# Attention with group norm over 32 batches: first input tile in two transfers, last products reordered, last output in four parts

## What is computed

```
q = conv1x1(Wq, bq, y);  k = conv1x1(Wk, bk, y);  v = conv1x1(Wv, bv, x)
scores = einsum('bhdl,bhel->bhde', q, k) / sqrt(E)        # per head, 16 x 16
attn = softmax(scores, axis=-1)
out = einsum('bhde,bhel->bhdl', attn, v).reshape(B, E, Lx)
o = conv1x1(Wo, bo, out) + x
o_hat = (o - mean(o)) * rsqrt(var(o) + EPS)               # over all of a batch
return o_hat * gn_w + gn_b
```

## Time and profile before

| What | us |
|---|---|
| Median of three executions | 175.67 |
| Lowest and highest of them | 175.47, 176.19 |
| The profiled execution, its own time | 175.87 |
| Its span in the trace | 174.1 |
| Busy in the span: PE, DVE, ACT, POOL | 163.0, 151.8, 135.8, 112.4 |

### The profile page before, as it was taken

One profiled execution on the slowest core, in us unless ns is written; L12 is line 12 of the kernel. 1 busy time (PEld: TensorE's weight loads), 2 busy tenths in 40 slices (PEclk: granted clock), 3 DMA queues, 4 the chain that ended last, 5 costly groups with the idle time before them and its releaser, 6 DMA issues. The chain is left out here.

```text
span 174.1 us, 4168 instructions
## 1 busy us (share of the span) xinstructions
PE 163.0 (94%) x997; PEld 129.2 (74%) x997; DVE 151.8 (87%) x555; ACT 135.8 (78%) x356; POOL 112.4 (65%) x166
## 2 busy tenths in 40 slices
PE   7989999999999999999999999999999999999730
PEld 7877888877777888877777778888777777785410
DVE  1786999999998999999999999999999999976551
ACT  4656588998878888798888888888988888776442
POOL 3287677877866777776787677767778777741020
PEclk9999999999999999999999999999999999999995
DMA  6998778999899999989999999999999866622223
GB/s 206 409 416 339 254 224 322 328 334 334 279 355 336 311 330 321 332 308 342 334 314 325 356 324 326 313 333 330 330 339 327 297 237 241 242 121 120 121 115 126
DMA packets 14265, 50.70 MB, mean 291 GB/s; under 512 B 1712, under 2 KB 1712, under 8 KB 14256
## 3 DMA queue, kind: packets, MB, share of 16 engines
q1 hardware_dynamic: 13968, 50.34, 81.0%
q10 hardware_dynamic: 288, 0.27, 0.5%
HBM read 33.82 MB, written 16.78 MB: 291 GB/s over the span
## 5 line engine op out<-in xcount | busy, mean ns | idle before, releaser
L514 PE MATMUL o_ps<-x_sb,m_sb 128*128 128x512 f32 x128 | 63.1, 615 | 0.0
L431 DVE TENSOR_TENSOR hl_sb<-y_sb,hl_sb 128x512 fp32r<-128x512 f32 x64 | 47.9, 749 | 1.7 <-ACT hl_sb L326 1.0
L271 POOL TENSOR_TENSOR rstd<-veps,nhalf 128x1 f32<-128x1 f32 x32 | 28.2, 882 | 24.5 <-DVE veps L436 24.5
L326 ACT CAST hl_sb<-y_sb 128x512 fp32r<-128x512 f32 x64 | 39.5, 620 | 1.8 <-DMA y_sb<-in_ctx_dram 1.8
L514 PE MATMUL g_ps<-hl_sb 128*128 128x258 f32 x256 | 38.6, 293 | 0.0
L366 ACT ACTIVATE out_sb<-o_ps,shift,gain 128x1024 f32<-128x1024 f32 (+1 forms) x32 | 38.3, 1197 | 0.1
L300 POOL TENSOR_TENSOR lsuma<-hl_sb 128x256 f32<-128x256 f32 x31 | 23.2, 749 | 22.9 <-DVE hl_sb L431 22.9
L514 PEld LDWEIGHTS o_ps<-x_sb,m_sb 128*128 128x128 f32 x128 | 22.1, 191 | 14.9 <-issue 14.0
L514 PEld LDWEIGHTS g_ps<-hl_sb 128*128 128x128 f32 x256 | 32.8, 190 | 0.0
L321 ACT ACTIVATE a_sb<-sc_sb,smin 128x128 f32<-128x128 f32 x32 | 12.9, 402 | 16.8 <-DVE smin L422 16.7
L287 POOL TENSOR_TENSOR lsum<-lsuma,lsumb 128x256 f32<-128x256 f32 x31 | 22.8, 737 | 4.1
(11 more groups left out here) (64 smaller groups left out, 297.6 us busy)
## 6 DMA issues: line engine op xcount, KB each, us to landing
y_sb<-in_ctx_dram SPq DMA_DIRECT2D x32, 512.0 KB, 5.1
x_sb<-in_x_dram SPq DMA_DIRECT2D x32, 512.0 KB, 5.6
out_dram<-out_sb SPq DMA_DIRECT2D x31, 512.0 KB, 4.8
out_dram<-out_sb SPq DMA_DIRECT2D x2, 256.0 KB, 2.2
w_in<-in_weights_dram ACTq DMA_DIRECT2D x1, 256.0 KB, 5.4
cols<-in_columns_dram ACTq DMA_DIRECT2D x1, 3.0 KB, 3.3
```

What stands on the lines that cost most here:

```text
L271: nc.gpsimd.tensor_tensor(rstd[:, h1:h1 + 1], veps[:, h1:h1 + 1], nhalf[:, :], ALU.pow).then_inc(rstd_ready, 1)
L326: nc.scalar.copy(hl_sb[:, k, chunks, 0:C], y_sb[:, k, chunks, :]).then_inc(h_ready, 1)
L431: nc.vector.tensor_tensor(hl_sb[:, ky, chunks, C:2 * C], y_sb[:, ky, chunks, :], hl_sb[:, ky, chunks, 0:C].bitcast(F32), ALU.subtract).the ...
L514: return nc.tensor.matmul(dst, lhsT, rhs, start=start, stop=stop, **more)
```

## The change

It alters six things:

1. The first `y` tile arrives in two transfers of 256 KB, by columns; the first has a semaphore of its own, `y_first`. ACT rounds the first half on the first, and waits for the second before the second half.
2. `w_in` is issued by SP behind the second `y` tile, instead of by ACT. DVE makes `wqT` in step 2, behind the rest of the second half of tile 1.
3. One warm-up product less, and no two idle products behind the row product.
4. In step 2, DVE makes `k0` behind `p_sb` instead of ahead of it.
5. In step 34, PE puts batch 31's `softmax_product` between the two x products of batch 30, the folded product behind them, and the first x product of batch 31 ahead of batch 30's `mean`. In step 35 it runs batch 31's second x product ahead of batch 30's `variance`, and DVE makes `veps` between the two statistics instead of ahead of both.
6. ACT and DVE each normalise the last batch in two quarters of 256 columns, and SP sends four transfers of 128 KB, in the order ACT, DVE, ACT, DVE.

```
-WARM_UP = 8
+WARM_UP = 7
...
-            for k in range(UNROLL):
+            part = HALF
+            sp.dma_start(y_slot(0)[:, 0:part], batch_y(0)[:, 0:part]).then_inc(y_first, 16)
+            sp.dma_start(y_slot(0)[:, part:L], batch_y(0)[:, part:L]).then_inc(y_in[0], 16)
+            sp.dma_start(y_slot(1), batch_y(1)).then_inc(y_in[1], 16)
+            sp.dma_start(w_in[:, :, :].rearrange("p w c -> p (w c)"), weights).then_inc(w_loaded, 16)
+            for k in range(2, UNROLL):
                 sp.dma_start(y_slot(k), batch_y(k)).then_inc(y_in[k], 16)
...
-                    for half, done in ((0, normed), (1, normed_dve)):
-                        part = slice(half * HALF, (half + 1) * HALF)
-                        sp.wait_ge(done, B if half == 0 else 1)
+                    for j in range(2):
+                        part = slice(j * QUARTER, (j + 1) * QUARTER)
+                        sp.wait_ge(normed, B + j)
+                        sp.dma_start(batch(out, B - 1)[:, part], out_sb[:, ko, part]).then_inc(out_done[ko], 16)
+                        part = slice(HALF + j * QUARTER, HALF + (j + 1) * QUARTER)
+                        sp.wait_ge(normed_dve, 1 + j)
                         sp.dma_start(batch(out, B - 1)[:, part], out_sb[:, ko, part]).then_inc(out_done[ko], 16)
...
-            act.dma_start(w_in[:, :, :].rearrange("p w c -> p (w c)"), weights).then_inc(w_loaded, 16)
...
-                if has(t, 5):
+                if has(t, 5) and not is_step(t, RUSH + 1):
                     variance()
...
                     nc.vector.bn_stats(bn[:, h, 0, :], o_ps[:, h, 0:HALF])
+                    if is_step(t, RUSH + 1):
+                        variance()
...
-            keep_busy(FILL)
```

More of the change, by code:

```diff
@@ L328, in step @@
                 if has(t, 0):
-                    act.wait_ge(y_in[k], slot_count(t0, k, 0))
+                    if is_step(t, 0):
+                        act.wait_ge(y_first, 16)
+                    else:
+                        act.wait_ge(y_in[k], slot_count(t0, k, 0))
                     if exists(t, 4):
@@ L364, in step @@
                         act.wait_ge(out_done[ko], slot_count(t0, k, 9))
-                    part = slice(0, HALF if is_step(t, LAST) else L)
-                    nc.scalar.activation(out_sb[:, ko, part], o_ps[:, h1, part], ACT.Identity,
-                                         bias=shift[:, h1:h1 + 1], scale=gain[:, h1:h1 + 1]).then_inc(normed, 1)
+                    parts = (slice(0, QUARTER), slice(QUARTER, HALF)) if is_step(t, LAST) else (slice(0, L),)
+                    for part in parts:
+                        nc.scalar.activation(out_sb[:, ko, part], o_ps[:, h1, part], ACT.Identity,
+                                             bias=shift[:, h1:h1 + 1], scale=gain[:, h1:h1 + 1]).then_inc(normed, 1)
                 ahead = is_step(t, 0) or is_step(t, 1)
                 if ahead:
+                    if is_step(t, 0):
+                        act.wait_ge(y_in[k], 16)
                     round_half(1)
@@ L441, in step @@
                     rest_half(-1, 1)
+                if is_step(t, 2):
+                    dve.wait_ge(w_loaded, 16)
+                    nc.vector.tensor_scalar(wqT[:, :], w_in[:, 0, :], -SCALE, None, ALU.mult).then_inc(const_dve, 1)
                 if has(t, 2):
@@ L470, in step @@
                                                    in1=p_ps, op0=ALU.mult, op1=ALU.add).then_inc(p_copied, 1)
+                if is_step(t, 2):
+                    nc.vector.scalar_tensor_tensor(out=k0[:, :], in0=bkB[:, :], scalar=bq_col[:, :],
+                                                   in1=mask[:, :, :].rearrange("p h d -> p (h d)"),
+                                                   op0=ALU.mult, op1=ALU.add).then_inc(const_dve, 1)
                 if has(t, 4):
@@ L500, in step @@
                     dve.wait_ge(out_done[ko], slot_count(t0, k, 9))
-                    nc.vector.tensor_scalar(out_sb[:, ko, HALF:L], o_ps[:, h1, HALF:L], gain[:, h1:h1 + 1],
-                                            shift[:, h1:h1 + 1], ALU.mult, ALU.add).then_inc(normed_dve, 1)
+                    for part in (slice(HALF, HALF + QUARTER), slice(HALF + QUARTER, L)):
+                        nc.vector.tensor_scalar(out_sb[:, ko, part], o_ps[:, h1, part], gain[:, h1:h1 + 1],
+                                                shift[:, h1:h1 + 1], ALU.mult, ALU.add).then_inc(normed_dve, 1)
             step(0, 0)
             step(0, 1)
-            dve.wait_ge(w_loaded, 16)
-            nc.vector.tensor_scalar(wqT[:, :], w_in[:, 0, :], -SCALE, None, ALU.mult).then_inc(const_dve, 1)
             pipeline(dve, step, begin=2)
@@ L609, in step @@
                     last.then_inc(hl_ready, 1)
-                if has(t, 3):
-                    pe.wait_ge(r_copied, t - 2)
-                    product(m_ps[:, 0:E], wv, r_sb[:, :])
-                    product(m_ps[:, E:E + 1], r_sb[:, :], bv).then_inc(m_ready, 1)
+                if has(t, 3) and not is_step(t, RUSH):
+                    folded_product()
                 if has(t, 4):
```

43 lines of the change are left out of this document (27 added, 16 removed).

## The result

The changed kernel takes 177.53 us (median of 6 runs, 176.85 to 179.52) beside 175.66 us for the kernel before (6 runs, 175.46 to 176.19). The ratio is 1.0095, 95% interval 1.0060 to 1.0129: **slower by about 1%**, where 175.1 was forecast with a range to 175.7.

What follows compares the result with a forecast made beforehand. PE alone bounds the gapless middle, so only start and end can gain. Profiled: 175.87 - 0.65 (start) + 0.05 (steps 34 and 35) + 0.0 (last output) = 175.27; from the median, 175.67 - 0.6, rounded to 175.1 us; range 174.4 to 175.7.

Steps and rivals of the forecast that it cites:

- `cols` and tile 0: Start, transfers: first half of tile 0 on ACT at 3.45, 0.6 us sooner; `cols` on DVE at 3.6 instead of 4.24.
- The rival of an unmoved `cols`: Start: `cols` stays at 4.24, only the idle passes are saved, -0.43 us, 175.3; chance 0.13.
- The start of PE: Row product at 4.2, Gram from 5.2, four passes at the lower clock; products with ones at 6.6 instead of 7.28, -0.65 us.
- the first rival: Start: PE's clock is up before 5.2, so 7.28 becomes 6.2, -1.1 us, 174.6 to 174.8; chance 0.20.
- The chain of step 1: Ones, `b2_sb`, transpose, `g_sb` and second Gram keep their old lengths, so it adds nothing to the sum.
- Tile 1: Start, ACT: with the row product 0.57 us sooner, tile 1 is cast at 5.8 instead of 6.36.
- The third rival: Start: thinner PE work makes the clock rise only after the second Gram, +2.6 - 0.6 us, 177.7; chance 0.06.
- Steps 34 and 35: New order near the end: gain in front is lost in DVE's queue, +0.05 us, between -0.1 and +0.15.
- The last output: Four transfers: issue +0.6, transfer -0.3, old queueing of halves some 0.3; sum 0.0 us, between -0.2 and +0.3.
- `k0`, `wqT`, `w_in`: Moves at the start: `w_in` and `wqT` cost nothing; `k0` costs 0 to 0.3 us, taken as 0.

Runs made afterwards that it cites:

- e15: Kernel before with tile 0 cut in two by partitions (rows of 4 KB), ACT waiting for both parts: 178.54 us, ratio 1.0101.
- e3: Kernel before with tile 0 in two transfers by columns and the weights on SP behind tile 1: 175.82 us, ratio 0.9991.
- e8: Changed kernel with eight warm-up products, the idle products back and the last output in two halves: 176.33 us, ratio 1.0050.
- e6: Kernel before with only tile 0 in two transfers by columns, weights left on ACT: 176.24 us, ratio 1.0042.
- e1: Changed kernel with eight warm-up products and the idle products behind the row product again: 177.04 us, ratio 1.0072.
- e13: Changed kernel with four idle products behind the ones products of step 1, where PE paused: 177.33 us, ratio 1.0089.
- e2: Kernel before with seven warm-up products instead of eight and no two idle products: 175.38 us, three of 12 runs at 178.01 to 179.23.
- e10: Changed kernel with tile 0 in one transfer again and `k0` and `wqT` in their old places: 175.73 us, ratio 1.0010.
- e4: Kernel before with only the new order of steps 34 and 35: 175.71 us, ratio 0.9991.
- e5: Kernel before with only the last output in four parts: 176.38 us, ratio 1.0028.
- e7: Kernel before with only the weights moved to SP behind tile 1: 175.71 us, ratio 1.0003.
- e14: Kernel before with the two idle products moved behind the ones products of step 1, plus the new order of steps 34 and 35: 175.26 us, ratio 0.9968.
- e9: Kernel before with the two idle products moved from behind the row product to behind the ones products of step 1: 175.45 us, ratio 0.9981.
- e11: Changed kernel with ACT copying `b2_sb` between its two casts of tile 1 in step 1: 177.91 us, ratio 1.0129.
- e12: Changed kernel with tile 1 issued by ACT behind `cols` instead of by SP: 177.65 us, ratio 1.0102.

## Why the prediction was wrong, point by point

- **`cols` and tile 0: right.** ACT's cast at 3.56 (3.45 forecast), `diag` at 3.74 (3.6), the row product at 4.28 (4.2). The rival of an unmoved `cols` is out. Why it moved is less sure than the forecast had it: in e15 `cols` had landed at 3.03, ahead of the first half of tile 0 (4.36), so it does not always wait for the tile's first transfer.
- **The start of PE: better than forecast.** The clock was up at 4.66, so the Gram was done sooner and the ones started at 6.20, not 6.6. That is the mechanism of the first rival (7.28 "becomes 6.2"), and the gain at this place is its 1.1 us.
- **The chain of step 1: the step that failed.** "Then the chain of step 1 (ones, `b2_sb`, transpose, `g_sb`, Gram 1) has its old lengths", and of `w_in` and `wqT` that "both cost nothing". From the ones to the second Gram it took 3.74 instead of 2.32, and the Gram 0.68 more. Three terms stood at nothing in the sum: the wait for `b2_sb` behind a late tile 1, `wqT` ahead of `g_sb`, and a clock that falls back.
- **Tile 1.** "The cast of tile 1 at 5.8 instead of 6.36" took for granted that the tile lands as before (5.52, which left 0.3 us of room). It was cast at 6.55. I had read the earlier trace rows for `cols` and the first half, not for the transfer behind them. That the split makes the tile late is shown: all eight kernels with tile 0 whole have it at 5.4 to 5.7, all eight cut by columns at 5.8 to 7.5. That this alone costs the time is not: e3 has it at 6.48 and is as fast as before. Why the engines trail is not shown. The rule in the Trainium skill's "DMA: Bandwidth & Descriptors", section "Rules for kernel authors", is about two transfers to disjoint partition halves, for which it advises one transfer over all 128 partitions. The prediction stretched it to halves by columns and weighed it for the first half alone, which did land 0.5 us sooner; the loss was in the transfer behind. For partition halves e15 bears it out: tile 0 came at 6.25 instead of 4.04.
- **In-order ACT.** The copy of `b2_sb`, which needs nothing of tile 1, is queued behind both its casts. I named this queue only for the case that the tile is there. It turns a late tile into a pause of PE of 0.76 (after, e8) or 1.39 (e6), and into none beyond the old 0.35 where the ones come late enough (e3, e1).
- **The clock.** The third rival, with a chance of 0.06, gave 177.7, nearly the measured 177.53, but by another course: it let the clock rise late. It rose early and fell back at 8.07, behind the pause; that the number is so near is luck. The argument against it, that PE's stream "stays unbroken to the end of the first Gram", was true, but the break came right behind. e13 has no low stretch with the pause filled, but its profiled execution had an early tile 1, so this is a hint and no proof. e6 and e8 show that a pause need not turn the clock (1.39 and 0.76 us, clock kept in the profiled execution), where PE had been given its idle products before. e2 shows that without the three products it can rise late: the third rival's course, seen in the one long execution that was profiled. That missing idle products and a pause together turn it in the changed kernel is argued; e10, without the idle products and with no longer pause than before, kept it. The edits done alone moved the median by -0.55 (e2), -0.11 (e3), -0.05 (e4) and +0.45 (e5), -0.26 in sum; the whole change moved it by +1.87. Missing from that sum are the moves of `k0` and `wqT`.
- **Steps 34 and 35.** Forecast +0.05, measured -0.19 and -0.18. `m_sb` came 0.23 later (0.3 forecast), the mean as forecast (4.70 behind batch 30's product). The term off is DVE's stretch from mean to `vrow`, 0.79 instead of 0.89, and `x` of batch 31 0.1 sooner than thought.
- **The last output.** Forecast 0.0, measured +0.48 and +0.45. The last issue was to come 0.6 later and its transfer to be 0.3 shorter. Measured are 0.76 and 0.31 (2.50 from issue to end, 2.81 before). The credit of "some 0.3" for the old queueing of the halves was invented: nothing in the earlier trace rows showed it.
- **`k0`, `wqT`, `w_in`: "both cost nothing" and "I take 0".** e7 gives the weights 0.0. `wqT` took 0.76 us on DVE in all six traces with the move, and 0.22 in ten of the eleven with it in its old place (e14: 0.78), so it was not "one short DVE instruction". The wait of DVE that was to cover it, 0.49 in before, was gone: the rest of tile 1 ended at 8.51 and the transpose had begun at 7.91. PE's wait for `g_sb` was 0.46 (e1), 0.79 (e8) and 0.30 (after). By e8 against e3 the two moves are worth up to 0.7; no run separates them.

What stays open: why the DMA engines trail; why the clock falls in one kernel and not in another; and how the loss divides between the late tile, the moves of `k0` and `wqT`, and the clock. e1 and e13 are 1.1 and 1.4 us slower than before without a low stretch in their traces. The four output parts are 0.45 of that, and the 0.6 to 0.7 between e3 and e8 could be most of the rest.

## What to carry to other kernels

When a transfer at the head of a queue is cut, look where the next ones land, and what an in-order engine has queued behind them: here a first half 0.5 us sooner made the next tile 0.3 to 2 us late. Whether that costs depends on the cover ahead of it (e3: none; the changed kernel, whose ones came 0.9 sooner: a pause). A small instruction moved "into a wait" is free only if the wait is still there after the change. Idle products did best where PE waits anyway (e9, e14), not removed (e2) and not in front of work that is ready (before). Four small stores at the end cost SP 0.4 us each, which was more than their shorter landing gave back.

## What was unexpected of the hardware

Cutting a 512 KB load in two left the first of the 16 DMA engines on time (5.1 to 5.4 us, but 6.05 in e6) and the last up to 2 us late, whichever queue the next load was in; cut by partitions instead, all 16 were late by the same 2 us. The TensorE clock, once up at 4.66 us, fell back to 1.2 GHz at 8.07 behind a pause of 0.76 us and stayed there to 11.49; in e11, e12 and e15 it fell as well (at 8.4, 8.1 and 9.7 us, each behind pauses of PE) and in the traces of e6, with a longer pause, and of e8 it did not. The recorded mean clock does not show a late rise: an execution of e2 at 178.25 us has 0.990. Nor do idle products rule a fall out: three of 107 executions of the kernel before, at 176.6 to 176.7 us, have a mean clock of 0.970 or 0.971, the others 0.982 or more. Leaving out three small products made three executions in twelve 2.6 to 3.9 us longer than the median (e2); with two of them put elsewhere and the third in its place there was none in 24 (e9, e14).
